# A decoder layer with 60 experts: the shared expert's second product is moved from ahead of the expert rounds to behind them

## The chip, the cores and the metric

One core of one Trainium2 chip. The time is that of one execution on the device, in microseconds (us), the median of several runs. All data are float32.

## What is computed

A pre-norm decoder layer on 8 sequences of 100 tokens of width 512: self-attention, cross-attention, and a mixture of experts. The change touches only the last part, where `x` is the normed input, 800 rows of 512:

```python
gu = x @ se_gate_up_w.T                       # shared expert, 2 x 1408 hidden
shared = silu(gu[:, :1408]) * gu[:, 1408:] @ se_down_w.T
shared = shared * sigmoid(x @ shared_gate_w.T)
weights, sel = top_k(softmax(x @ gate_w.T), 4)   # of 60 experts
for e in range(60):                           # 352 hidden each
    gu_e = x @ w13[e].T
    sparse += cw[:, e] * ((silu(gu_e[:, :352]) * gu_e[:, 352:]) @ w2[e].T)
out = residual + shared + sparse
```

"The second product" of the shared expert is the one with `se_down_w` (1408 to 512).

## The kernel before

The kernel is written engine by engine: each has one block of instructions in a fixed order, and they meet by semaphores alone. `L1120` is line 1120 of the kernel. After the attention part (two sequences a turn, four turns) come these stages.

**Shared expert, first product.** `shared_up(u)` on PE (L1062) for 22 units (11 chunks of 128 hidden by 2 halves of 400 tokens); ACT takes the silu (L1375), DVE multiplies into `hT_all` (L1884). Its weights `se_up` come in 11 loads by SP into three buffers (`load_up`, L471). Beside it DVE chooses the experts and gives each token a row in `xs_d` (`choose`, `sort`, `slots`); when `slots_ready` is given (L1872), POOL scatters the normed rows from `xn3` to `xs_d` with 32 indirect transfers (L727).

**Shared expert, second product.** PE waits for `sh_h`, `down_loaded`, `slots_ready`. With `w_down` as the weights and `hT_all` as the moving side it makes 8 groups (2 halves by 4 chunks of the output) of 11 matmuls, each of which the trace counts as two (L1120). ACT copies each group to `dnT` (L1422), PE transposes back to rows of tokens (L1114, `down_back`), DVE adds them, times the gate, to `acc` (L1899), which holds the residual. `acc` is loaded by L525 and `w_down` by L526, ahead of the fourth `se_up` load on SP's queue.

**Expert rounds.** 20 rounds of three experts. One has a tile of 128 rows ("single", k = 0), two share a tile, 64 rows each ("pair", k = 1). In a round PE does: gate/up of the pair (L1149), transposes of the next single rows (L1137), down of the single (L1176), transposes of hidden (L1164), gate/up of the next single (L1145), rows transposes, down of the pair (L1180), hidden transposes. Two rounds are one turn of a loop; the first transposes and gate/up stand ahead of it and the last round and a half behind. Experts alternate between two sets s = 0, 1 of three buffers (`w13_s[s][b]`, `w2_s[s][b]`); SP loads an expert in three transfers, 2112 KB together (L532 to L534), when the buffer's last reader is done (`y_full`). ACT loads the rows (L1379) and stores the results (L1399). Before the change PE's first rows transpose waits for DVE's adds (`dn_free`, L1201), and SP's `load_pair(1, 1)` waits for `dn_full` (L548), since these buffers lie over `hT_all`. Experts with more rows than a tile would go through an overflow block with a counter (L1219 and its like on the other engines); in this data it runs no turn.

**Gather.** POOL fetches the four result rows of each token with 32 indirect transfers (L738), into four slots of `xn3` that are free again when DVE has added them to `acc` with the token's weights (L1957). After the four of one sequence SP stores it (L576).

**Memory.** All of this lies in one arena of 51250 floats a partition, laid out by hand: `carve` gives out space, and resetting `top[0]` lays one tile over another.

Of the kernel before, what the change touches and what calls it, by code (L numbers as in the profile page):

```python
# [13 lines left out]
P = 128  # L14
# [106 lines left out]
def decoder_kernel(nc, x, ctxT, dcaT, W_attn, W_out, b_out, Wq, bq, Wkv, bkv, Wdca, bdca, norm, Wo, bo,  # L121
# [6 lines left out]
    with cm:  # L128
# [123 lines left out]
        xsT = [carve(DC, T) for _ in range(2)]  # L252
        s_sh = [carve(400) for _ in range(2)]
        xn3 = carve(B, D)
        oh = carve(B, E)
# [10 lines left out]
        w2_s[1][0] = carve(3, D)  # L266
        assert top[0] <= B * DC * S + 3 * DC * 2 * P
        top[0] = B * DC * S + 3 * DC * 2 * P
        dnT = arena[:, DC * 2 * I + 3 * D:DC * 2 * I + 3 * D + DC * 400].rearrange("p (a b) -> p a b", a=DC)
        assert DC * 2 * I + 3 * D + DC * 400 <= B * DC * S + 3 * DC * 2 * P  # L270
        for b in (1, 2):
            w13_s[1][b] = carve(DC, 2 * I)
            w2_s[1][b] = carve(3, D)
        assert top[0] <= B * DC * S + 3 * DC * 2 * P + MC * B * S
        top[0] = B * DC * S + 3 * DC * 2 * P + MC * B * S
# [3 lines left out]
        y_s = [carve(D) for _ in range(2)]  # L279
        top[0] = xs_at  # L280
# [73 lines left out]
        dn_full = sem("shared_down_full")  # L354
        dn_free = sem("shared_down_free")
        r_act = sem("router_exp")
# [60 lines left out]
        def _(sp):  # L417
# [146 lines left out]
            with sp.If(count > 0):  # L564
                with sp.Fori(0, NOV) as t:
                    with sp.If(count > t):
                        e = sp.value_load(ov_i[0:1, bass.ds(t, 1)], min_val=0, max_val=E - 1)
                        sp.wait_ge(o_y, t + 1)
                        sp.sem_inc(load_gate, 1)
                        sp.dma_start(w13_s[0][0], w13[e, :, :, :]).then_inc(o_w, 16)  # L570
                        sp.dma_start(xs_s[0][0], xs_d[bass.ds(t * T + TILES * T, T), :]).then_inc(o_w, 16)
                        sp.dma_start(w2_s[0][0][:, 0:2, :], w2[e, 0:256, :].rearrange("(p c) n -> p c n", c=2)).then_inc(o_w, 16)
                        sp.dma_start(w2_s[0][0][0:96, 2, :], w2[e, 256:I, :]).then_inc(o_w, 16)
            for b in range(B):
# [168 lines left out]
        def _(pe):  # L743
# [362 lines left out]
            pe.wait_ge(sh_h, UNITS)  # L1106
            pe.wait_ge(down_loaded, 16)
            pe.wait_ge(slots_ready, 1)

            def down_back(half):  # L1110
                pe.wait_ge(dnT_copied, 4 * (half + 1))
                for b in range(half * 4, half * 4 + 4):
                    for d in range(DC):
                        last = nc.tensor.transpose(ps[0:S, b, d * P:(d + 1) * P], dnT[:, d, (b % 4) * S:(b % 4 + 1) * S], ident[:])  # L1114
                    last.then_inc(dn_full, 1)

            for half in range(2):
                for d in range(DC):
                    for m in range(MC):
                        last = nc.tensor.matmul(ps[:, half * 4 + d, 0:400], w_down[:, m, d * P:(d + 1) * P],  # L1120
                                                hT_all[:, m, half * 400:(half + 1) * 400], start=(m == 0), stop=(m == MC - 1))
                    last.then_inc(dnT_full, 1)
                    if (half, d) == (1, 0):
                        down_back(0)
            down_back(1)


# [91 lines left out]
            with pe.If(count > 0):  # L1219
                with pe.Fori(0, NOV) as t:  # L1220
                    with pe.If(count > t):
                        pe.wait_ge(o_w, t * 64 + 64)
                        pe.wait_ge(o_yc, t + 1)
                        rows_products(xs_s[0][0]).then_inc(o_t, 1)
                        pe.wait_ge(o_tc, t + 1)
                        gate_up_products(0, 0).then_inc(o_g, 1)
# [3 lines left out]
                        down_products(0, 0).then_inc(o_y, 1)  # L1230


        @block.scalar
        def _(act):
# [181 lines left out]

            for half in range(2):
                for d in range(DC):
                    act.wait_ge(dnT_full, half * 4 + d + 1)
                    if half:  # L1420
                        act.wait_ge(dn_full, 4)
                    nc.scalar.activation(dnT[:, d, :], ps[:, half * 4 + d, 0:400], ACT.Copy).then_inc(dnT_copied, 1)  # L1422

            silu(0, 0)
# [15 lines left out]
            with act.If(count > 0):  # L1440
                with act.Fori(0, NOV) as t:
                    with act.If(count > t):
                        act.wait_ge(o_g, t + 1)
                        silu_part(0).then_inc(o_s, 1)
                        act.wait_ge(o_y, t + 2)
                        act.wait_ge(o_st, t * 16 + 1)
                        nc.scalar.activation(y_s[0], ps[:, 6, :], ACT.Copy).then_inc(o_yc, 1)
                        act.wait_ge(o_yc, t + 2)
                        act.dma_start(ys_d[bass.ds(t * T + TILES * T, T), :], y_s[0]).then_inc(o_st, 16)


        @block.vector
        def _(dve):
# [441 lines left out]

            dve.wait_ge(acc_loaded, 16)
            for b in range(B):
                dve.wait_ge(dn_full, b + 1)
                nc.vector.scalar_tensor_tensor(out=acc[0:S, b, :], in0=ps[0:S, b, :], scalar=rsm[0:S, 6, b, 2:3],  # L1899
                                               in1=acc[0:S, b, :], op0=ALU.mult, op1=ALU.add).then_inc(dn_free, 1)  # L1900

            def rows_T(k, turn):
# [40 lines left out]
            with dve.If(count > 0):  # L1943
                with dve.Fori(0, NOV) as t:
                    with dve.If(count > t):
# [5 lines left out]
                        hidden_T_part(0).then_inc(o_htc, 1)  # L1951
            dve.wait_ge(dn_free, B)
            for b in range(B):
                for k in range(TOPK):
                    n = b * TOPK + k
                    dve.wait_ge(gathered[n % 4], 16 * (n // 4 + 1))
                    ins = nc.vector.scalar_tensor_tensor(out=acc[0:S, b, :], in0=xn3[0:S, n % 4, :], scalar=rsm[0:S, 5, b, k:k + 1],  # L1957
                                                         in1=acc[0:S, b, :], op0=ALU.mult, op1=ALU.add)
                    ins.then_inc(added[n % 4], 1)
                    dve.wait_ge(added[n % 4], n // 4 + 1)  # L1960
                dve.sem_inc(out_ready, 1)

# [47 lines left out]
```

## Time and profile before

| | us |
|---|---|
| median of 3 timed runs | 1322.32 (1320.95 to 1324.74) |
| the profiled execution, its span | 1337.3 |
| PE busy in it | 1142.7 (85%) |
| first shared product, first to last matmul | 681.2 to 826.3 |
| second shared product | 827.0 to 890.7 |
| expert rounds | 890.5 to 1277.9 |
| gather and output | 1278.6 to 1337.3 |

Engines: PE = TensorE matmul, PEld its weight loads, DVE = VectorE, ACT = ScalarE, POOL = GpSimd, SP = SyncE, which here only issues transfers; "SPq", "ACTq" are the queues' issues. Times are us from the span's start. In brackets behind a row stands how long the engine was idle ahead of it, and what ended that; "issue" is idle time in which it waited for nothing that the profile shows. PEclk is the granted clock of TensorE as a share of 2.4 GHz. The DMA share is the mean busy share of 16 transfer engines; it can pass 1 a little. The profiled execution is 15 us longer than the median of the timed ones.

### The profile page before, as it was taken

What the parts mean: (1) busy time and instruction counts of PE and PEld (TensorE: products, weight loads), DVE (VectorE), ACT (ScalarE), POOL (GpSimd) and SP (SyncE); (2) the same over time, 40 slices, a digit from 0 to 9 for tenths busy, and PEclk for the clock granted to TensorE, in tenths of its full rate; (3) what the DMA queues carried; (4) which work ended last, traced back from release to release, by engine and by line L of the source; (5) the groups of instructions that cost most, each with busy time, mean ns of one, the idle gap of its engine ahead of it and who ended that gap; (6) DMA issues with size and microseconds to landing.
All of it is one profiled execution on the core that took longest, in us unless ns stands there. A gap on an engine that the chain in (4) does not pass through costs nothing.

```text
span 1337.3 us, 19386 instructions
## 1 busy us (share of the span) xinstructions
PE 1142.7 (85%) x5710; PEld 630.4 (47%) x5710; DVE 495.5 (37%) x1360; ACT 255.0 (19%) x796; POOL 397.3 (30%) x917
## 2 busy tenths in 40 slices
PE   2889899988999899898979988989988989989920
PEld 0444564446644466444645544555444544444500
DVE  7232755337552375525754601012111111211234
ACT  0141421324232241413321100001101110101100
POOL 3677206852088422884000170000000000000045
PEclk8999899899999899998989998999989998989965
DMA  9998001000100001002037286038999999999835
GB/s 313 333 394 308 1 21 32 22 1 2 32 21 22 0 2 50 3 1 85 1 89 193 74 260 229 3 115 327 385 377 375 383 379 382 384 385 387 326 112 149
DMA packets 76439, 232.73 MB, mean 174 GB/s; under 512 B 11346, under 2 KB 13750, under 8 KB 68670
## 3 DMA queue, kind: packets, MB, share of 16 engines
q1 hardware_dynamic: 58686, 197.55, 41.3%
q10 hardware_dynamic: 11520, 20.98, 4.4%
q0 software_dynamic: 6144, 13.13, 3.3%
q8 instruction: 42, 0.69, 0.2%
q14 instruction: 47, 0.39, 0.1%
HBM read 178.40 MB, written 53.22 MB: 173 GB/s over the span
## 4 chain that ended last, share of the span: by engine, by line
PE 46%; POOL 19%; issue 12%; DMA 11%; DVE 6%; SPq 2%; POOLq 2%; ACT 1%; DVEq 0%; ACTq 0%
PE ps L1062 8%; PE ps L1149 7%; PE ps L1145 6%; DMA arena<-in_w 5%; PE ps L1120 4%; POOL arena L667 4%; PE ps L791 4%; PE ps L1180 3%; PE ps L1176 3%; PE ps L946 2%; POOL arena L664 2%; DMA arena<-ys_d,slot_u 2%; DMA arena<-in_se_up 2%; POOL arena L689 2%; PE ps L926 2%
## 5 line engine op out<-in xcount | busy, mean ns | idle before, releaser
L791 PE MATMUL ps<-arena 128*100 128x512 f32 (+3 forms) x576 | 221.4, 537 | 6.3 <-ACT arena L1247 3.7
L738 POOL DMA_INDIRECT arena<-ys_d,slot_u x32 | 35.0, 1095 | 492.0 <-issue 487.5
L791 PEld LDWEIGHTS ps<-arena 128*100 128x100 f32 (+1 forms) x576 | 90.9, 178 | 114.0 <-issue 108.3
L1149 PE MATMUL ps<-arena 128*64 128x352 f32 x640 | 116.9, 525 | 29.0 <-issue 25.9
L1062 PE MATMUL ps<-arena 128*128 128x400 f32 x352 | 125.0, 514 | 15.6 <-issue 8.3
L873 PE MATMUL ps<-arena 128*100 128x512 f32 x256 | 114.5, 592 | 0.0
L1905 DVE COPY arena<-ps 128x512 f32<-128x512 f32 x40 | 27.7, 691 | 232.8 <-PE ps L1137 232.8
L1062 PEld LDWEIGHTS ps<-arena 128*128 128x128 f32 x352 | 68.4, 195 | 70.8 <-issue 20.5
L1145 PE MATMUL ps<-arena 128*128 128x352 f32 x320 | 98.0, 459 | 1.7 <-issue 1.7
L1149 PEld LDWEIGHTS ps<-arena 128*64 128x64 f32 x640 | 55.4, 156 | 82.9 <-issue 60.6
L1300 ACT ACTIVATE arena<-ps,arena 100x345 f32<-100x345 f32 x128 | 69.2, 546 | 113.4 <-DVE arena L1697 111.8
L1145 PEld LDWEIGHTS ps<-arena 128*128 128x128 f32 x320 | 59.2, 190 | 31.6 <-issue 1.9
L873 PEld LDWEIGHTS ps<-arena 128*100 128x100 f32 x256 | 42.0, 166 | 59.7 <-issue 57.3
L1697 DVE TENSOR_REDUCE arena<-ps 100x1 f32<-100x345 f32 x128 | 60.8, 507 | 24.0 <-PE ps L917 23.5
L946 PE MATMUL ps<-zero 128*128 128x200 f32 x320 | 67.3, 342 | 0.0
L1392 ACT ACTIVATE arena<-ps 128x352 f32<-128x352 f32 x40 | 18.6, 464 | 238.3 <-PE ps L1149 145.6
L727 POOL DMA_INDIRECT xs_d<-arena,slot_u x32 | 31.9, 997 | 100.3 <-DVE ov_i L1872 90.9
L1701 DVE COPY arena<-ps 115x400 f32<-115x400 f32 x92 | 52.4, 569 | 23.4 <-PE ps L926 23.0
L667 POOL TENSOR_TENSOR arena<-arena 115x256 f32<-115x256 f32 (+7 forms) x128 | 57.8, 452 | 10.0
L926 PE MATMUL ps<-ident,arena 100*115 100x100 f32 x384 | 52.4, 273 | 9.3 <-DVE arena L1701 9.1
L1120 PE MATMUL ps<-arena 128*128 128x400 f32 x176 | 59.5, 500 | 0.7 <-DVE arena L1884 0.7
L1180 PE MATMUL ps<-arena 128*64 128x512 f32 (+1 forms) x240 | 56.0, 601 | 0.7 <-DVE arena L1921 0.7
(214 smaller groups left out, 1517.3 us busy)
## 6 DMA issues: line engine op xcount, KB each, us to landing
arena<-in_w SPq DMA_DIRECT2D x60, 1408.0 KB, 11.5
arena<-in_w SPq DMA_DIRECT2D x60, 512.0 KB, 12.1
xs_d<-zero SPq DMA_DIRECT2D x5, 3328.0 KB, 26.3
arena<-in_w SPq DMA_DIRECT2D x60, 192.0 KB, 13.7
arena<-xs_d ACTq DMA_DIRECT2D x40, 256.0 KB, 8.0
ys_d<-arena ACTq DMA_DIRECT2D x40, 256.0 KB, 7.7
ys_d<-zero SPq DMA_DIRECT2D x2, 3328.0 KB, 24.3
arena<-in_se_up SPq DMA_DIRECT2D x11, 512.0 KB
```

Source lines behind the costliest of these rows:

```text
L667: then(nc.gpsimd.tensor_tensor(s3[:, :, 0:w], s3[:, :, 0:w], s3[:, :, w:2 * w], ALU.add))
L791: last = nc.tensor.matmul(ps[0:m, k, 0:cols[1] - cols[0]], lhs(c), w[:, c, cols[0]:cols[1]], start=(c == 0), stop=(c == n_c - 1))
L873: last = nc.tensor.matmul(ps[0:S, j, :], cT[c % 2][:, g, :], w_out[:, c * G + g, :], start=(c == 0 and g == 0), stop=(c == KV - 1 and g == ...
L926: last = nc.tensor.transpose(ps[0:LC, k, r * S:(r + 1) * S], xp[(4 * t + r) % NP_][0:S, c * LC:(c + 1) * LC], ident[0:S, 0:S])
L946: nc.tensor.matmul(ps[:, 6 + j, 0:2 * S], zero[:, 0:P], zero[:, 0:2 * S], start=False, stop=False)
L1062: last = nc.tensor.matmul(ps[:, (u % 3) * 2 + gu, 0:400].rearrange("p (a b) -> p a b", a=4), se_w[m % 3][:, c, gu * P:(gu + 1) * P], tok, ...
L1120: last = nc.tensor.matmul(ps[:, half * 4 + d, 0:400], w_down[:, m, d * P:(d + 1) * P], hT_all[:, m, half * 400:(half + 1) * 400], start=(m ...
L1145: last = nc.tensor.matmul(ps[:, 1 + gu, 0:I], xsT[0][:, c, :], w13_s[s][0][:, c, at:at + I], start=(c == 0), stop=(c == DC - 1))
L1149: last = nc.tensor.matmul(ps[half * HALF:(half + 1) * HALF, 3 + gu, 0:I], xsT[1][:, c, half * HALF:(half + 1) * HALF], w13_s[s][1 + half][ ...
L1180: last = nc.tensor.matmul(ps[half * HALF:(half + 1) * HALF, 7, :], hT[1][0:w, n, half * HALF:(half + 1) * HALF], w2_s[s][1 + half][0:w, n, :],
L1300: nc.scalar.activation(xp[(4 * t + r) % NP_][0:S, :], ps[0:S, k, 0:LM], ACT.Exp, bias=xnm[0:S, j, h:h + 1], scale=1.0, accum_out=xsum[0:S, ...
L1697: nc.vector.tensor_reduce(xnm[0:S, j, h:h + 1], ps[0:S, k, 0:LM], AX, ALU.max, negate=True).then_inc(xmax_ready.sem, 1)
```

## The change

The second product with its transposes moves on PE behind the rounds and the overflow block; ACT's copies to `dnT` move likewise. DVE's `acc` additions of it are interleaved with the gathered ones: image b's gathered rows, then the shared part of image b - 4, and at the end those of 4 to 7. `dn_free` is gone. The loads: `acc` goes out behind the last expert's load, `w_down` once both `y_full` say that round 18 is done. In the arena, `w_down` now lies over set 0's buffers (the single's, and the start of the first pair buffer); the set 1 pair buffers move off `hT_all`: one has space of its own, the other lies over `s_sh` and `xn3`. So `load_expert(1, 1, ...)` can go out at once behind the first round's, and `load_expert(1, 2, ...)` when all units of `sh_h` are done and all rows are scattered. The overflow block uses set 1's single buffer instead of set 0's. Arithmetic and the number of instructions are the same.

```diff
@@ arena
+        xT3_end = top[0]
         hT_all = carve(MC, B * S)
-        w_down = carve(MC, D)
         acc = carve(B, D)
+        down_at = top[0]
         for b in range(3):
             w13_s[0][b] = carve(DC, 2 * I)
             w2_s[0][b] = carve(3, D)
+        w13_s[1][1] = carve(DC, 2 * I)
+        w2_s[1][1] = carve(3, D)
...
+        top[0] = xn3_at
+        w13_s[1][2] = carve(DC, 2 * I)
+        w2_s[1][2] = carve(3, D)
+        assert top[0] <= xn3_end
+        top[0] = down_at
+        w_down = carve(MC, D)
@@ sync
             sp.dma_start(xn3[0:S], xn3_d.rearrange("b s d -> s b d")).then_inc(xn3_loaded, 16)
-            sp.dma_start(acc[0:S], x2_d.rearrange("b s d -> s b d")).then_inc(acc_loaded, 16)
-            sp.dma_start(w_down, se_down.rearrange("(c p) n -> p c n", p=P)).then_inc(down_loaded, 16)
             for m in range(3, MC):
                 load_up(m)
...
             load_pair(0, 0)
+            load_expert(1, 1, 2 + SINGLES)
+
             sp.wait_ge(sh_up, UNITS)
             load_single(1, 1)
-            sp.wait_ge(dn_full, B)
-            load_pair(1, 1)
+
+            sp.wait_ge(sh_h, UNITS)
+            sp.wait_ge(scattered, 16 * B * TOPK)
+            load_expert(1, 2, 2 + SINGLES + 1)
             with sp.Fori(0, ROUNDS // 2 - 1) as ii:
...
+
+            sp.dma_start(acc[0:S], x2_d.rearrange("b s d -> s b d")).then_inc(acc_loaded, 16)
+
+            sp.wait_ge(y_full[0], ROUNDS)
+            sp.wait_ge(y_full[1], ROUNDS)
+            sp.dma_start(w_down, se_down.rearrange("(c p) n -> p c n", p=P)).then_inc(down_loaded, 16)
@@ tensor
             pe.wait_ge(sh_h, UNITS)
-            pe.wait_ge(down_loaded, 16)
             pe.wait_ge(slots_ready, 1)
-            def down_back(half):
...
-            down_back(1)
@@
-            pe.wait_ge(dn_free, 4)
             transpose_rows(0, 0, 0, 0)
             gate_up(0, 0, 0, 0)
             transpose_rows(1, 0, 0, 0)
-            pe.wait_ge(dn_free, B)
             transpose_hidden(0, 0)
@@ behind the overflow block
+            pe.wait_ge(down_loaded, 16)
+            def down_back(half):
...
+            down_back(1)
@@ vector, behind the overflow block
-            dve.wait_ge(dn_free, B)
-            for b in range(B):
+            dve.wait_ge(acc_loaded, 16)
+
+            def add_gathered(b):
                 for k in range(TOPK):
...
+            def add_shared(b):
+                dve.wait_ge(dn_full, b + 1)
+                nc.vector.scalar_tensor_tensor(out=acc[0:S, b, :], in0=ps[0:S, b, :], scalar=rsm[0:S, 6, b, 2:3],
+                                               in1=acc[0:S, b, :], op0=ALU.mult, op1=ALU.add).then_inc(out_ready, 1)
+
+            for b in range(B):
+                add_gathered(b)
+                if b >= 4:
+                    add_shared(b - 4)
+            for b in range(4, B):
+                add_shared(b)
```

## Rows read from the trace of the kernel before

**Rows 1.** The page's slices: busy tenths in 40 equal slices.
```profile
PE   2889899988999899898979988989988989989920
DMA  9998001000100001002037286038999999999835
```

**Rows 2.** Busy time by stretch (columns: PE, PEld, DVE, ACT, POOL; clock, DMA, GB/s).
```profile
850.00:900.00 50.00, 46.37 (x168) 27.89 (x166) 7.23 (x12) 2.99 (x7) 0.00 (x0) 1.00 0.15 56
905.00:910.00 5.00, 5.00 (x21) 2.98 (x20) 1.80 (x5) 1.06 (x2) 0.00 (x0) 1.00 0.33 91
1200.00:1250.00 50.00, 46.92 (x212) 24.49 (x212) 9.87 (x29) 5.90 (x11) 0.00 (x0) 0.97 1.03 381
1265.00:1270.00 5.00, 4.08 (x29) 2.40 (x31) 0.62 (x2) 0.59 (x1) 0.00 (x0) 1.00 0.19 67
1300.00:1338.00 38.00, 0.00 (x0) 0.00 (x0) 16.52 (x22) 0.00 (x0) 21.94 (x20) 0.50 0.52 147
```

**Rows 3.** The chain that ended last, from 690 us on (start, length, what).
```profile
702.39 24.70 DMA arena<-in_se_up
...
826.40 0.58 DVE arena L1884
827.03 37.21 PE ps L1120 x110
...
865.99 22.18 PE ps L1120 x66
...
888.75 1.95 PE ps L1114 x16
...
1333.64 0.75 DVE arena L1957
```

**Rows 4.** Timeline of PE, 665 to 850 us: the unit behind the rank products.
```profile
727.13 5.64 PE L1062 MATMUL ps<-arena 128*128 128x400 f32 x16 [0.45 <-DMA arena<-in_se_up]
```

**Rows 5.** Timeline around the start of the expert rounds.
```profile
823.65 1.83 ACTq L1379 DMA_DIRECT2D arena<-xs_d  x4
...
889.43 2.73 DVE L1899 SCALAR_TENSOR_TENSOR arena<-ps,arena 100x512 f32<-100x512 f32 x4 [21.91 <-PE ps L1114]
...
892.85 4.97 PE L1145 MATMUL ps<-arena 128*128 128x352 f32 x16 [1.72 <-issue]
```

**Rows 6.** The tile xs_d, 800 to 900 us: its six row loads.
```profile
DMA to landing us min/median/max: 2.6/4.1/8.8
```

**Rows 7.** Timelines of SP and of PE in the expert rounds.
```profile
909.48 0.35 SPq L532 DMA_DIRECT2D arena<-in_w  x1
...
917.40 0.34 SPq L532 DMA_DIRECT2D arena<-in_w  x1
...
934.18 4.95 PE L1149 MATMUL ps<-arena 128*64 128x352 f32 x32 [0.50 <-DMA arena<-in_w]
...
993.52 7.35 PE L1149 MATMUL ps<-arena 128*64 128x352 f32 x32 [3.72 <-issue]
...
1252.16 0.34 SPq L534 DMA_DIRECT2D arena<-in_w  x1
```

**Rows 8.** PE's waits, 905 to 1275 us (total, times, longest).
```profile
PE ps L1149 <- issue: 25.9, 10, 3.7
```

**Rows 9.** Timeline of the end of the rounds and the first gather.
```profile
1275.11 2.80 PE L1180 MATMUL ps<-arena 128*64 128x512 f32 x12 [0.71 <-DVE arena L1921]
...
1282.53 1.05 POOL L738 DMA_INDIRECT arena<-ys_d,slot_u  x1 [479.58 <-issue]
```

**Rows 10.** By stretch again, while acc and w_down are loaded.
```profile
704.00:706.00 2.00, 2.00 (x7) 1.13 (x6) 0.78 (x3) 1.63 (x4) 0.00 (x0) 1.00 0.96 200
718.00:720.00 2.00, 2.00 (x26) 2.00 (x24) 0.88 (x3) 0.00 (x0) 0.00 (x0) 1.00 0.92 345
```

**Rows 11.** The load of w_down: from issue to landing.
```profile
DMA to landing us min/median/max: 32.2/32.2/32.2
```

**Rows 12.** Timeline of DVE, 740 to 905 us, around the engine stall.
```profile
806.88 1.13 DVE L1884 TENSOR_TENSOR arena<-arena,ps 128x400 f32<-128x400 f32 x2 [22.64 <-remote]
```

More of the change, by code:

```diff
@@ L252, in decoder_kernel @@
         xsT = [carve(DC, T) for _ in range(2)]
+        xn3_at = top[0]
         s_sh = [carve(400) for _ in range(2)]
         xn3 = carve(B, D)
+        xn3_end = top[0]
         oh = carve(B, E)
@@ L260, in decoder_kernel @@
         rsm = carve(8, B, 8)
-        top[0] = 0
-        w13_s[1][0] = carve(DC, 2 * I)
[L266 to L275, printed above, removed]
         sl = [carve(I) for _ in range(2)]
@@ L279, in decoder_kernel @@
         y_s = [carve(D) for _ in range(2)]
+        top[0] = 0
+        w13_s[1][0] = carve(DC, 2 * I)
+        w2_s[1][0] = carve(3, D)
+        dnT = carve(DC, 400)
+        assert top[0] <= xT3_end
+        top[0] = xn3_at
[4 more added lines that the diff above has]
+        w_down = carve(MC, D)
         top[0] = xs_at
@@ L354, in decoder_kernel @@
         dn_full = sem("shared_down_full")
-        dn_free = sem("shared_down_free")
         r_act = sem("router_exp")
@@ L1106, in _ @@
             pe.wait_ge(sh_h, UNITS)
-            pe.wait_ge(down_loaded, 16)
             pe.wait_ge(slots_ready, 1)
-            def down_back(half):
[L1111 to L1124, printed above, removed]
-            down_back(1)
             def transpose_rows(k, s, turn, j):
@@ L1229, in _ @@
                         pe.wait_ge(o_htc, t + 1)
-                        down_products(0, 0).then_inc(o_y, 1)
+                        down_products(0, 1).then_inc(o_y, 1)
+                        pe.wait_ge(o_yc, t + 2)
+            pe.wait_ge(down_loaded, 16)
+            def down_back(half):
+                pe.wait_ge(dnT_copied, 4 * (half + 1))
+                for b in range(half * 4, half * 4 + 4):
+                    for d in range(DC):
+                        last = nc.tensor.transpose(ps[0:S, b, d * P:(d + 1) * P], dnT[:, d, (b % 4) * S:(b % 4 + 1) * S], ident[:])
+                    last.then_inc(dn_full, 1)
+            for half in range(2):
+                for d in range(DC):
+                    for m in range(MC):
+                        last = nc.tensor.matmul(ps[:, half * 4 + d, 0:400], w_down[:, m, d * P:(d + 1) * P],
+                                                hT_all[:, m, half * 400:(half + 1) * 400], start=(m == 0), stop=(m == MC - 1))
+                    last.then_inc(dnT_full, 1)
+                    if (half, d) == (1, 0):
+                        down_back(0)
+            down_back(1)
         @block.scalar
@@ L1415, in round_ @@
                 store(1, i)
[L1417 to L1422, printed above, removed]
             silu(0, 0)
@@ L1449, in _ @@
                         act.dma_start(ys_d[bass.ds(t * T + TILES * T, T), :], y_s[0]).then_inc(o_st, 16)
+            for half in range(2):
+                for d in range(DC):
+                    act.wait_ge(dnT_full, half * 4 + d + 1)
+                    if half:
+                        act.wait_ge(dn_full, 4)
+                    nc.scalar.activation(dnT[:, d, :], ps[:, half * 4 + d, 0:400], ACT.Copy).then_inc(dnT_copied, 1)
         @block.vector
@@ L1894, in _ @@
             run(router)
-            dve.wait_ge(acc_loaded, 16)
-            for b in range(B):
-                dve.wait_ge(dn_full, b + 1)
-                nc.vector.scalar_tensor_tensor(out=acc[0:S, b, :], in0=ps[0:S, b, :], scalar=rsm[0:S, 6, b, 2:3],
-                                               in1=acc[0:S, b, :], op0=ALU.mult, op1=ALU.add).then_inc(dn_free, 1)
             def rows_T(k, turn):
@@ L1951, in _ @@
                         hidden_T_part(0).then_inc(o_htc, 1)
-            dve.wait_ge(dn_free, B)
-            for b in range(B):
+            dve.wait_ge(acc_loaded, 16)
+            def add_gathered(b):
                 for k in range(TOPK):
@@ L1956, in _ @@
                     dve.wait_ge(gathered[n % 4], 16 * (n // 4 + 1))
-                    ins = nc.vector.scalar_tensor_tensor(out=acc[0:S, b, :], in0=xn3[0:S, n % 4, :], scalar=rsm[0:S, 5, b, k:k + 1],
-                                                         in1=acc[0:S, b, :], op0=ALU.mult, op1=ALU.add)
-                    ins.then_inc(added[n % 4], 1)
+                    nc.vector.scalar_tensor_tensor(out=acc[0:S, b, :], in0=xn3[0:S, n % 4, :], scalar=rsm[0:S, 5, b, k:k + 1],
+                                                   in1=acc[0:S, b, :], op0=ALU.mult, op1=ALU.add).then_inc(added[n % 4], 1)
                     dve.wait_ge(added[n % 4], n // 4 + 1)
-                dve.sem_inc(out_ready, 1)
+            def add_shared(b):
[8 more added lines that the diff above has]
+                add_shared(b)
 def kernel(x, ctx_1024, L0_attn_W_attn, L0_attn_W_out, L0_attn_b_out, L0_xattn_Wq, L0_xattn_bq, L0_xattn_Wk, L0_xattn_bk,
```

8 lines of the change are left out of this document (4 added, 4 removed).

## The prediction

> **What bounds the kernel now.** I read the slices of the page first, then the table by stretch, then the chain of waits, then the timelines of the places that the change touches. In the 40 slices of 33.4 us [rows 1] the reader is to see two holes: DMA at 0 and 3 in the 26th and 27th slice (836 to 903 us), and PE at 2 and 0 in the last two. By stretch [rows 2], 850 to 900 us has 46.4 us of PE work and 56 GB/s of transfers; 1200 to 1250 has 46.9 us of PE work and 381 GB/s, DMA share 1.03; 1300 to 1338 has no PE work. So three stages in a row have three limits: the shared down product runs on PE alone, the expert rounds run at what the DMA engines carry (with PE close behind), the gather at the end runs on POOL, DMA and DVE with PE empty. The chain goes through all three one after the other. The down product fills 827.03 to 890.70 = 63.7 us of it (110 and 66 matmuls and, between and behind them, two lots of 16 transposes, of which the second has its row) [rows 3], and the first expert row transpose follows at once. Behind the last expert product, which ends at 1277.9, 59.4 us of gather and store remain to the span's end at 1337.3 [rows 9]. The change moves the 63.7 us from a place where PE is the chain to one where PE is idle. In the best case nearly all of it is hidden by the gather; what isn't is the sum below. All instants are those of the profile of before.
>
> **Part 1, the early loads.** SP no longer issues acc (1600 KB) and w_down (2816 KB) at 692.9 to 702.4. Behind them the fourth se_up load was late, but the chain's 24.70 us of DMA [rows 3] is its flight, not PE's wait: PE idled 0.45 us for it [rows 4]. Gain between 0 and 0.5 us; I take 0.
>
> **Part 2, where the rounds start.** After the change PE needs three things for its first transpose: the last hidden (DVE, which starts at 826.40 and takes 0.58 [rows 3]: 827.0), slots_ready (long there: the scatters run on it from 761.6) and its rows. ACT issues the row loads at 823.65 already now, landing in 2.6, 4.1 or 8.8 us (shortest, median, longest of six such loads) [rows 5, 6]: at 826.3, 827.7 or 832.5. I take the median, since the queues are nearly empty then. In the kernel before, the first L1145 came at 892.85, just behind a DVE copy that itself had to wait until the last adds L1899 ended at 889.43 + 2.73 = 892.16 [rows 5]. Now transposes 0.6, copy 0.7, 0.1 of passing on: 827.7 + 1.4 = 829.1. Shift 892.85 - 829.1 = 63.7; with the longest landing 59. Some "issue" idle at this first run through the code is not excluded, so I take 63. SP's added waits are harmless: load (1,1) goes out behind the first three experts, at about 808.5; (1,2) waits for the last hidden and the scatters (POOL's last at 802), so about 828.5. Behind that wait on SP stand only round 2's loads, which need a round to finish first. A pair load issued from 917.40 on was in use at 934.18 with DMA full [rows 7]; (1,2), issued at 828.5, is wanted at about 853.
>
> **Part 3, the rounds.** Before, pair (1,1) went out from 891.45 and was there long before its use at 916.85; the DMA share of 905 to 910 was 0.33 [rows 2], so the queues ran empty before round 2's first load at 909.48 [rows 7]. From there to the end they are full. So loading (1,1) and (1,2) early takes bytes out of a place that had room, and doesn't shorten the full part: 20 rounds keep their length, 0. Bounds: -0.5 (the 0.50 us wait at 934.18 [rows 7]) and +3 (one more loop-head stall like those of [rows 7, 8]). The acc load stands on SP's queue behind the last expert load (issued 1252.2 [rows 7]), and delays none.
>
> **Part 4, the weights of the moved product.** w_down lies over expert buffers of the even rounds, so SP waits for y_full of round 18: L1180 ends at about 1264.9, and the issue follows at 1265.3 to 1265.8. The expert loads drain at about 1265.9 (67 GB/s in 1265 to 1270 is 0.34 MB [rows 2]). Then acc and w_down stand in the queue: 4.52 MB. What they took before: w_down landed 32.2 us after its issue at 693.62 [rows 11], so at 725.8, with xn3 and acc ahead of it; the rate was 200 GB/s at 704 to 706 although the engines' share was 0.96, and 345 at best [rows 10]. The 2 us stretches from 692 on, of which two stand there, add up to the 1.84 MB ahead of acc at about 703.7, so the two took 22.1 us. 1265.9 + 22.1 = 1288. The ends: 1265.9 + 4.52 MB at 381 GB/s [rows 2] = 1277.8, and the full 32.2 us from issue = 1297.5. I take 1287.5, since the nearest row is the same two loads, and se_up traffic that was mixed in then is gone. PE is ready at 1278.6 plus the walk past the overflow block; it waits about 9 us.
>
> **Part 5, the moved product.** 63.7 us of its own [rows 3]; its covers there (ACT copies of 0.5 us behind each group of 22) come with it. PE has been idle 9 us, and its granted clock falls to 0.50 (1.2 GHz) when it idles [rows 2]. At the loop heads the 32 matmuls L1149 behind 3.7 us of idle take 7.35 us, against 4.95 at full clock [rows 7]: +2.4. End of PE: 1287.5 + 63.7 + 2.4 = 1353.6. The last add trails the last transpose by 892.16 - 890.70 = 1.5 [rows 3, 5]; the last output store takes what it takes now, 1337.3 - (1333.64 + 0.75) = 2.9 [rows 3]. End: 1358.0, 20.7 behind the old one.
>
> **Part 6, the gather beside it.** DVE adds the shared part of image b - 4 behind the gathered rows of image b. Images 0 to 4 are gathered by about 1318. dn_full of image 0 comes at 1287.5 + 2.4 + 37.2 + 0.5 = 1327.6, so DVE stands there some 10 us, and queued behind it are images 5 to 7 and POOL's gathers, which go at most four ahead of DVE. The four of image 5 have landed; the eight others need two turns of the ring, each about 6.5 us (four gathers of 1.05 us and 0.3 between them [rows 9], then the last one's landing): 1344 with the adds. That is 9 us before PE ends, so the stall is hidden. What ACT and DVE do for the product costs no more than there: it follows PE. The last y store (256 KB, 2.0 us alone) now shares the engines with w_down; 2 us more there shift the gather only, inside those 9 us.
>
> **Sum.** -63 + 20.7 = -42.3. On the profiled execution 1337.3 - 42.3 = 1295.0. The median of the timed runs is 1322.3, 15.0 below the profiled span. None of my terms rests on what the profiling adds, as far as I can tell, so I carry the difference over: 1322.3 - 42.3 = 1280.0.
>
> **The rivals.**
> (a) The weights land early. If acc and w_down move at the rounds' rate they are there at 1277.8 and PE runs on. That takes 9 us of waiting and 2.4 us of slow clock away, since 0.71 us of idle before L1180 cost no clock (2.80 us, as in the other rounds) [rows 9]; but PE's walk past the overflow block is no longer hidden, priced by the loop heads' 2.9 to 3.7 us of "issue" (25.9 us in ten places, 3.7 the longest) [rows 8]: 1280 - 9 - 2.4 + 3 = about 1272. For: w2 is loaded in short rows too and the rounds reach 381 GB/s. Against: [rows 10], these very transfers.
> The Trainium skill, "DMA: Bandwidth & Descriptors", section "Anatomy of one DMA", gives about 2 us plus bytes over 436 GB/s for one transfer; by it the two would be there near 1278, this rival. No row here shows such a rate for these two.
> The skill's "Runtime: NRT & Kernel Launch", section "Instruction fetch mechanics", says that a taken branch outside the fetched pages stalls the engine; that fits the loop heads' "issue" idle and would count against placing work behind the overflow branch, but only in this rival, where nothing covers it.
> (b) The weights land late, as 32.2 us behind their issue: PE starts at 1297.5, +10: 1290. For: gather and y store share the engines. Against: xn3 isn't ahead of them now.
> (c) The engine stall of 784 to 806 grows. DVE idled 22.64 us there for something "remote", and two hidden products came together at 806.88 [rows 12], where they were due every 5.4 us (16 matmuls at 37.21 / 110 us [rows 3]) behind the one of 783.7, at 789 and 794.5: about 12 us lost, while transfers were dense. The fourth expert load now keeps the queues dense to about 820, and the same may recur there, or in the gather: +12, 1292. For: it coincides with dense transfers. Against: 704 to 706 was dense too (share 0.96 [rows 10]) and PE ran through.
> (d) The same stall goes away, as SP's early transfers are fewer: -12, 1268. For: it isn't in the data flow. Against: the engines' code ahead of it is unchanged.
> (e) Slower: the moved product stays at the low clock. It sits beside the gather, PE starts cold, and at 1.2 GHz for its whole length it takes 127 instead of 66: 1341, 19 us above the old time. It decides from the point where the product takes over 66 + 42 = 108 us. For: the clock is 0.50 all through the gather now. Against: PE is idle there now; behind a loop head 32 matmuls take 7.35 us, not the 9.9 that half the clock would make of all of them [rows 7], so PE gets its clock back within them, and here it starts with denser ones.
> (f) The change doesn't do what it says: the first rounds still wait for something late (rows, or pair (1,2)), and half of the shift is lost: 1311. Against: every releaser I found is there by 832.5.
>
> **How the numbers follow.** Forecast 0.52, (a) 0.14, (b) 0.12, (c) 0.09, (d) 0.07, (e) 0.03, (f) 0.03. The forecast's own spread is 6 us either way (row landing, 4 us; weights within the bounds). The range holds the forecast, (a), (b) and (c) and most of (d): 1265 to 1296. A measurement of this kernel tells about 0.3%, 4 us, from no change. Faster: all but (e) and what of (f) is worse than half: 0.95. Same: 0.02. Slower: 0.03.
>
> **What would show it.** The first L1145 near 829; L1149 of round 0 to 3 with the same spacing as now; the w_down landing 20 to 24 us behind the last expert load's end, and a PE idle of 7 to 11 us put down to it; the product 66 us long with the clock at 0.50 for its first 3 to 5 us; the chain of the last 75 us on PE, not on POOL; DVE idle some 10 us for dn_full after image 4. I am wrong if the rounds get longer, if the gather ends last, or if PE shows "issue" idle inside the product.

## The result, and the profile after

| | us |
|---|---|
| before, median of 4 | 1321.89 (1320.95 to 1324.74) |
| after, median of 4 | 1289.76 (1282.66 to 1291.61) |
| ratio | 0.9743, 95% interval 0.9709 to 0.9777 |
| profiled execution of after, its span | 1286.5 (before: 1337.3) |

The change gains 32.1 us. 42.3 were forecast: 1280.0, range 1265 to 1296. The span of the profiled execution fell by 50.8 us, much more than the median. That gap is the first thing to explain, and a part of the forecast's error lies in it.

I cut each profile at three instants: first L1062 of the shared expert (called L1073 after the change), first gate/up of the rounds (L1145; L1137), end of the last expert product (L1180; L1172).

| profile | first shared matmul at | to first gate/up | rounds | tail | span |
|---|---|---|---|---|---|
| before | 681.2 | 211.7 | 385.0 | 59.4 | 1337.3 |
| after | 675.0 | 148.4 | 387.7 | 75.4 | 1286.5 |
| difference | -6.2 | -63.3 | +2.7 | +16.0 | -50.8 |
| forecast | 0 | -63 | 0 | +20.7 | -42.3 |

By this table the forecast's terms look right, and the start exact to 0.3 us. It isn't: the chain of after shows an item that the forecast didn't have. First the chain (start, length, what; "..." stands where lines are left out):

```profile
727.29 80.81 PE ps L1073 x240
808.19 0.58 DVE arena L1894
808.77 12.73 issue
821.51 1.08 PE ps L1129 x4
...
1193.37 22.07 DMA arena<-in_se_down
...
1215.48 38.90 PE ps L1235 x110
1254.38 1.75 PE ps L1229 x16
1256.13 22.18 PE ps L1235 x66
```

Against [rows 3]: the shared product's last group is followed by 12.73 us in which PE does nothing, put down to "issue". At the end the chain is w_down's load and then the product (L1235), no longer the gather. The engine timelines of the same two places:

```profile
811.99 1.87 ACTq L1389 DMA_DIRECT2D arena<-xs_d  x4
821.51 1.08 PE L1129 MATMUL ps<-ident,arena 128*128 128x128 f32 x4 [13.42 <-issue]
823.42 6.74 PE L1137 MATMUL ps<-arena 128*128 128x352 f32 x16 [0.83 <-issue]
...
1215.48 7.00 PE L1235 MATMUL ps<-arena 128*128 128x400 f32 x15 [4.39 <-DMA arena<-in_se_down]
```

These answer to [rows 5]. ACT's last silu ended at 805.9 and nothing of its own was due, yet it issued the row loads at 811.99: its program waits there for the scatters, and for nothing else. POOL had issued the last of those by 796.8, but in 810 to 812 us seven of their packets (q0) were still moving beside the expert loads (q1); the columns are packets, MB and share:

```profile
q1 hardware_dynamic: 73, 0.60, 92.2%
q0 software_dynamic: 7, 0.02, 2.6%
```

And the row loads themselves took, in 800 to 822 us,

```profile
DMA to landing us min/median/max: 9.3/11.8/12.8
```

where [rows 6] had 2.6, 4.1 and 8.8 (in the same profile the four loads of the start alone took 2.6 to 4.2). So PE's idle is a wait for rows, although the profile doesn't say so. The stretches show why (columns as in [rows 2]):

```profile
800.00:805.00 5.00, 5.00 (x17) 2.81 (x16) 0.57 (x1) 0.50 (x1) 0.00 (x0) 1.00 1.04 408
805.00:810.00 5.00, 3.08 (x10) 1.42 (x8) 0.57 (x1) 0.50 (x1) 0.00 (x0) 1.00 0.98 385
815.00:820.00 5.00, 0.00 (x0) 0.00 (x0) 0.00 (x0) 0.00 (x0) 0.00 (x0) 0.50 1.05 352
825.00:830.00 5.00, 5.00 (x15) 2.93 (x15) 0.00 (x0) 0.00 (x0) 0.00 (x0) 0.80 0.02 8
```

The transfer engines are full from 785 to 825, and PE idles inside that; when PE works again they are empty. PE's clock fell to 0.50, so the first gate/up took 6.74 us instead of 4.97 [rows 5].

### The profile page after: what moved, and what is told of

The parts are those of the page before. It is cut to its first block, busy times and chain, and to the rows that moved or that the text cites. A ratio compares the mean times of both kernels' runs of the same rounds, so it can differ in the third digit from the quotient of the medians.

```text
span 1286.5 us, 19385 instructions
## 1 busy us (share of the span) xinstructions
PE 1141.3 (89%) x5710; PEld 627.8 (49%) x5710; DVE 496.4 (39%) x1360; ACT 254.3 (20%) x796; POOL 394.6 (31%) x917
## 3 DMA queue, kind: packets, MB, share of 16 engines
q1 hardware_dynamic: 58686, 197.55, 42.3%
## 4 chain that ended last, share of the span: by engine, by line
PE 48%; POOL 18%; issue 12%; DMA 11%; DVE 6%; SPq 2%; POOLq 2%; ACT 1%; DVEq 0%; ACTq 0%
PE ps L1073 9%; PE ps L1141 7%; DMA arena<-in_w 6%; PE ps L1137 6%; PE ps L1235 5%; POOL arena L678 4%; PE ps L802 4%; PE ps L1172 3%; PE ps L1168 3%; PE ps L957 3%; POOL arena L675 2%; POOL arena L700 2%; PE ps L937 2%; DMA arena<-in_se_down 2%; POOL arena L689 2%
## 5 line engine op out<-in xcount | busy, mean ns | idle before, releaser
L1141 PE MATMUL ps<-arena 128*64 128x352 f32 x640 | 117.2, 527 | 29.8 <-issue 15.1
L1073 PE MATMUL ps<-arena 128*128 128x400 f32 x352 | 122.0, 509 | 6.6 <-DMA arena<-xT_d 5.7
L1137 PE MATMUL ps<-arena 128*128 128x352 f32 x320 | 99.8, 466 | 0.8 <-issue 0.8
L1073 PEld LDWEIGHTS ps<-arena 128*128 128x128 f32 x352 | 67.9, 194 | 59.3 <-issue 8.5
L1141 PEld LDWEIGHTS ps<-arena 128*64 128x64 f32 x640 | 53.5, 157 | 85.7 <-issue 71.7
L1137 PEld LDWEIGHTS ps<-arena 128*128 128x128 f32 x320 | 60.2, 193 | 31.7 <-issue 2.7
L1402 ACT ACTIVATE arena<-ps 128x352 f32<-128x352 f32 x40 | 18.5, 463 | 254.3 <-PE ps L1141 146.5
L1235 PE MATMUL ps<-arena 128*128 128x400 f32 x176 | 61.2, 510 | 4.4 <-DMA arena<-in_se_down 4.4
L738 POOL DMA_INDIRECT xs_d<-arena,slot_u x32 | 31.8, 995 | 100.5 <-DVE ov_i L1882 91.1
L1172 PE MATMUL ps<-arena 128*64 128x512 f32 (+1 forms) x240 | 56.0, 601 | 0.7 <-DVE arena L1925 0.7
```

Source lines behind the costliest of these rows:

```text
L1073: last = nc.tensor.matmul(ps[:, (u % 3) * 2 + gu, 0:400].rearrange("p (a b) -> p a b", a=4), se_w[m % 3][:, c, gu * P:(gu + 1) * P], tok, ...
L1137: last = nc.tensor.matmul(ps[:, 1 + gu, 0:I], xsT[0][:, c, :], w13_s[s][0][:, c, at:at + I], start=(c == 0), stop=(c == DC - 1))
L1141: last = nc.tensor.matmul(ps[half * HALF:(half + 1) * HALF, 3 + gu, 0:I], xsT[1][:, c, half * HALF:(half + 1) * HALF], w13_s[s][1 + half][ ...
L1172: last = nc.tensor.matmul(ps[half * HALF:(half + 1) * HALF, 7, :], hT[1][0:w, n, half * HALF:(half + 1) * HALF], w2_s[s][1 + half][0:w, n, :],
```

## The experiments

All ratios are against the kernel before, run on the same chip. "start" is the time from the first shared matmul to the first gate/up, "wait" PE's idle before the moved product. (1,0), (1,1) and (1,2) are the three experts of round 1: the single and the two of the pair. "1/11 product" leaves out ten of the eleven chunks of the second product.

| run | ratio (95% interval) | start | rounds | tail | wait | span |
|---|---|---|---|---|---|---|
| before, again | 1.0008 (0.997 to 1.0047) | 200.1 | 384.4 | 56.9 | | 1318.3 |
| before, 1/11 product | 0.9583 (0.952 to 0.9646) | 146.3 | 380.9 | 59.8 | | 1261.7 |
| after, again | 0.974 (0.9716 to 0.9765) | 144.6 | 383.6 | 78.8 | 8.2 | 1282.4 |
| after, 1/11 product | 0.9651 (0.9594 to 0.9708) | 145.4 | 384.2 | 64.9 | 3.5 | 1270.9 |
| rows first | 0.9698 (0.9624 to 0.9772) | 136.0 | 387.8 | 80.0 | 8.0 | 1282.0 |
| (1,1) behind the scatters | 0.9727 (0.9699 to 0.9756) | 135.3 | 389.7 | 78.0 | 6.6 | 1281.7 |
| (1,0), (1,2) behind the rows | 0.9706 (0.9684 to 0.9729) | 141.2 | 377.6 | 78.9 | 7.4 | 1274.8 |
| acc early | 0.9683 (0.965 to 0.9715) | 148.6 | 380.7 | 71.4 | 2.1 | 1276.5 |
| acc early, again | 0.969 (0.9653 to 0.9727) | 149.1 | 381.0 | 71.4 | 2.1 | 1279.6 |
| rows first, acc early | 0.9722 (0.9699 to 0.9745) | 136.0 | 397.4 | 71.3 | 2.1 | 1281.2 |
| (1,0), (1,2) behind the rows, acc early | 0.9726 (0.97 to 0.9753) | 141.6 | 396.5 | 72.9 | 2.1 | 1287.6 |
| (1,1) behind the scatters, acc early | 0.9722 (0.9686 to 0.9758) | 134.8 | 398.8 | 72.9 | 2.1 | 1279.4 |

**1. Was the profile of before a usual one?** The kernel before, unchanged.

> The kernel before, unchanged, for a second profile. Theory S (the profile on which the prediction rested carried a stall of the engines of about 12 us at 784 to 806, and some 6 us more ahead of it, which the timed runs don't have): the span is 1318 to 1325 now, DVE has no idle of 22.64 us for something remote in the first shared product, and from the first L1062 matmul to the first L1145 of the rounds it takes about 199 us, not 211.6. Theory N (the stall belongs to the kernel before, and the 10 us missing from the forecast are lost elsewhere): span near 1337, 211.6 us again. The ratio is 1 by both.

Measured: span 1318.3, start 200.1 us. Theory S holds for the start: 11.6 us of the 211.7 in the profile on which the forecast rests were a stall that this execution lacks. The 56 timed executions of the kernel before lie between 1313.9 and 1332.4 us, and in every later run the profiled span is 1.8 to 2.1 us below the time of the same execution. So the 1337.3 us were an unusually long execution, and not something that profiling adds. ACT, PE and the stretches at the hand-over, in this second profile of before:

```profile
807.81 0.50 ACT L1375 ACTIVATE arena<-ps 128x400 f32<-128x400 f32 x1 [4.87 <-PE ps L1062]
809.17 1.83 ACTq L1379 DMA_DIRECT2D arena<-xs_d  x4
811.19 29.15 PE L1120 MATMUL ps<-arena 128*128 128x400 f32 x86 [0.73 <-DVE arena L1884]
```
```profile
800.00:805.00 5.00, 5.00 (x17) 2.81 (x16) 0.39 (x1) 0.50 (x1) 0.00 (x0) 1.00 1.01 405
805.00:810.00 5.00, 5.00 (x17) 2.77 (x15) 0.57 (x1) 0.50 (x1) 0.00 (x0) 1.00 0.35 137
```

The reader is to see that the queues run dry at about 807 and the rows are issued at 809.17, 2 us later. In the first profile the stall of [rows 12] had held PE and ACT back by 12 us while the transfers went on, so the rows went out at 823.65 [rows 5] into queues empty since 815. When nothing stalls, the kernel has 2 us of such margin. The second product hid that too: PE needs the rows only 64 us later.

**2. What the product cost where it stood.** Before, with one chunk of eleven (the rest is left out); `range(MC)` becomes `range(1)` in the loop around L1120.

> The kernel before with the second shared product cut to 1 of its 11 chunks of hidden (16 matmuls instead of 176; its transposes, copies and adds stay). Part of the computation is left out. It measures what PE's time there is worth where it stood. If all of it is on the path, 160 matmuls at 0.338 us = 54 us are gained: ratio 0.959, and everything behind is as before. Theory Q (transfers hold the start of the rounds once the product is gone) says the same here, since 9 us of transposes and copies are left as cover: between 48 and 54. A gain under 45 would say that the rounds can't start earlier at all.

Measured: 56.1 us less (1265.94 against 1322.06), against 54 of matmul time; start 146.3 instead of 200.1, 53.8 less. All of what was left out was on the path, and a start of 146 us was reached with transposes, copies and adds still in it, and three early experts instead of four.

**3. What it costs where it stands now.** The same cut in the changed kernel.

> The changed kernel with the same cut, 1 of 11 chunks, where the product stands now, behind the rounds. Part of the computation is left out. If the gather hides most of the product, the end falls back to the gather: tail from the last expert product to the end 59.4 us as before plus some 3 us for a gather that starts later behind w_down, so 62 to 63 instead of 75.4: 13 us less than the changed kernel, ratio 0.965. If nothing is hidden (PE's work there holds the gather up by the adds), 54 us less: 0.934.

Measured: 1275.1, 14.7 us below the changed kernel's 1289.8 in its own runs and about 10.7 below its second series (1285.8); the tail is 64.9 us against 75.4 and 78.8. So of the 54 us, 11 to 15 show behind the rounds and 39 to 43 are hidden by the gather. 62 to 63 were expected for the tail; 64.9 came. POOL's first gather starts 6.0 us behind the last expert product (1212.04 against 1206.0), where it took 4.6 before: the last y store shares the engines with w_down. The other runs bear that out: 6.0 to 8.1 us in the six profiles with acc behind the rounds, and 4.6 in the five with acc early (experiments 6 and 7), where w_down had landed before the last expert product ended.

**4. Scatters, rows and expert loads at the start of the rounds.** SP issues round 1's experts only when the first rows are there:

```diff
-            load_expert(1, 1, 2 + SINGLES)
             sp.wait_ge(sh_up, UNITS)
-            load_single(1, 1)
             sp.wait_ge(sh_h, UNITS)
             sp.wait_ge(scattered, 16 * B * TOPK)
+            sp.wait_ge(xs_loaded[1][0], 16)
+            load_single(1, 1)
+            load_expert(1, 1, 2 + SINGLES)
             load_expert(1, 2, 2 + SINGLES + 1)
```

> The changed kernel, but SP issues the three experts of round 1 only when the rows of round 0 have landed (waits on the last hidden, the scatters and the row load of the pair). Theory Q (the 13.4 us of PE idle ahead of the rounds are scatters and row loads that wait among dense expert transfers): 2.16 MB less stand beside the scatters and 4.3 MB less beside the rows, so ACT's row loads go out at about 806 instead of 812 and land in 3 to 4 us; PE starts 9 to 11 us earlier, ratio 0.967 to 0.969. Theory F (the idle is the engines' own stall at new code, not the transfers): no change, ratio 0.976. Against it: if the experts of round 1 now come late, PE waits for them in round 1 and the gain is lost there.

Measured: start 136.0, 12.4 us less. ACT and PE, and PE's waits from 830 us on:

```profile
809.85 1.83 ACTq L1388 DMA_DIRECT2D arena<-xs_d  x4
812.76 0.63 PE L1128 MATMUL ps<-ident,arena 128*128 128x128 f32 x4 [1.48 <-DVE arena L1893]
```
```profile
PE ps L1140 <- DMA arena<-in_w: 27.7, 8, 4.5
PE ps L1234 <- DMA arena<-in_se_down: 8.0, 1, 8.0
```

The 13.4 us of idle became 1.5, and ACT issued 0.7 us behind its last silu instead of 6.1: theory Q is shown, theory F is out. But the median is 1284.6, and the ratio 0.9698 isn't clear of the changed kernel's. Counted from the first shared matmul, the end came at 603.8 us, against 611.5 and 607.0 in the two profiles of the changed kernel: 12.4 or 8.6 us gained at the start, 7.7 or 3.2 left at the end. PE's waits put down to expert weights grew from 14.7 and 18.6 to 27.7 us, and the wait for w_down is as long as ever. About half was given back. The transfers that the start no longer carries are made up in the rounds: 387.8 us at a mean of 376 GB/s are 146 MB, against 387.7 us at 363 GB/s, 141 MB, in the changed kernel. So the column "rounds" doesn't compare like with like where experts are loaded later.

**5. Which of the loads does it.** Expert (1,1) alone moved behind the scatters, `load_expert(1, 1, ...)` next to (1,2):

> The changed kernel, but expert (1,1) is loaded behind the scatters, together with (1,2), instead of ahead of them; (1,0) stays at the end of the first shared product. Theory Q1 (the fourth early expert delays the scatters, and ACT's row loads wait for these): the row loads go out at about 809 instead of 812. They still stand behind (1,0) and beside two more experts, so they land 9 to 11 us later: PE starts about 3 us earlier, and first shared product to first gate/up takes 145 us instead of 148.4. If the fourth expert alone were the cause, 136 as in the run where all three wait.

Measured: 135.3, not 145. My split was wrong. Without the fourth expert the scatters end at about the same time as ACT's last silu (809.0); the rows go out at 809.60, ahead of SP's (1,0) at 811.86, and the two terms vanish together:

```profile
809.60 1.84 ACTq L1388 DMA_DIRECT2D arena<-xs_d  x4
...
812.59 0.63 PE L1128 MATMUL ps<-ident,arena 128*128 128x128 f32 x4 [1.48 <-DVE arena L1893]
```

The other way round, (1,1) early and (1,0), (1,2) behind the rows:

> The changed kernel, but (1,0) and (1,2) are issued when the pair's first rows have landed; (1,1) goes out early as in the changed kernel. Theory Q2 (the row loads themselves stand among expert transfers): they go out at 812 as now, since the scatters are still late, but land in 3 to 4 us instead of 9 to 13; PE starts about 6 us earlier: 142 us instead of 148.4.

Measured: 141.2. The rows, still issued late behind the scatters (813.62, 5.6 us behind the last silu), land in 2.6, 3.6 and 4.5 us instead of 9.3, 11.8 and 12.8, and PE's idle is 6.2 us instead of 13.4:

```profile
816.43 1.09 PE L1129 MATMUL ps<-ident,arena 128*128 128x128 f32 x4 [6.22 <-issue]
```

Both halves are shown: the fourth early expert delays the scatters, for which the rows wait, and then the loads (1,0) and (1,2) delay the rows. The first causes the second. All profiles agree on the first half: ACT issues the rows 5.2 to 7.4 us behind its last silu in the seven with (1,1) early, and 0.1 to 0.7 in the four with (1,1) later.

**6. The load of acc.** Back at its old place, behind xn3; only w_down stays behind the rounds.

> The changed kernel with the acc load back at its old place, behind xn3; only w_down is loaded behind the rounds. Theory D (the end of the rounds is bound by transfers up to the landing of w_down, acc being part of them): w_down lands 14 to 15 us behind its issue instead of 22.1, so it is there before PE needs it: PE's 4.4 us of wait and some 2 us of slow clock go, 5 to 6 us less than the changed kernel, ratio 0.970. The early acc costs 0.5 us at most. If w_down's landing doesn't depend on acc: no change.

> The changed kernel with the acc load at its old place, a second time: the one step beside the change that looked better than it (0.9683), and a second profile of it. The profiles so far have a pace of the rounds from 19.05 to 20.2 us at 366 to 390 GB/s, with 19.15 in the first run of this kernel and 19.9 to 20.2 in its three relatives that also load acc early. If the pace belongs to the kernel: 19.1 to 19.2 us again, rounds of 380 us, ratio 0.967 to 0.969. If it belongs to the execution: anywhere in that span, and the ratio between 0.968 and 0.973; the tail is 71 to 72 us with a product wait of 2 us by both, since that is what acc early changes.

Measured, twice: w_down lands 11.9 and 11.6 us behind its issue instead of 22.1, PE waits 2.1 us both times (put down to "issue"; I take it for PE's own walk past the overflow block, which rival (a) priced at 3), and the tail is 71.4 us both times. Ratios 0.9683 and 0.969; medians 1278.1 and 1279.8. In the first profile PE's wait, and the time to landing of w_down:

```profile
PE ps L1234 <- issue: 2.1, 1, 2.1
```
```profile
DMA to landing us min/median/max: 11.9/11.9/11.9
```

By its medians this is the best kernel of the study, some 6 to 12 us below the changed one. The intervals overlap (0.9653 to 0.9727 and 0.9716 to 0.9765 in the second pair), so I take the sign as likely, and as shown only the 4 to 7 us of the tail.

**7. Do the two steps add up?** Three combinations of 4, 5 and 6.

> Both: round 1's experts behind the first rows, and acc early. In the run with the rows first alone, PE started the rounds 12.4 us earlier, but waited 8.0 us for w_down at the end instead of 4.4, and rounds had 27.7 us of waits for weights instead of 14.7. Theory D: without acc these 8 us are gone, 1284.6 - 8 = 1277, ratio 0.964, better than both kernels. If the end is bound by other transfers, w_down lands as late as now and the ratio stays 0.970.

> The changed kernel with (1,0) and (1,2) behind the first rows, (1,1) early, and acc at its old place. Apart these gave starts of 141.2 us (instead of 148.4) and a product wait of 2.1 us (instead of 4.4) with a ratio of 0.9706 and 0.9683. If they add up: start 141, wait 2, ratio 0.963 to 0.966, better than both kernels. If the end of the rounds is set by the bytes to move from 777 on (the transfers never pause, so an earlier start of PE only turns into waits for weights), it stays at 0.968 to 0.970, as with acc early alone.

> The changed kernel with (1,1) behind the scatters and acc at its old place. Start 135 us (measured apart), product wait 2. If starts and tails add up freely, ratio 0.960 to 0.963. By the bytes theory the earlier start is given back in the rounds, as in the run with the rows first and acc early (397 us of rounds at 369 GB/s instead of 388 us at 384): 0.968 to 0.972.

They don't. Starts of 136.0, 141.6 and 134.8 and waits of 2.1 came as expected, but the rounds took 397.4, 396.5 and 398.8 us, and the ratios are 0.9722, 0.9726 and 0.9722. The pace of the transfers in 920 to 1190 us, changed kernel, rows first with acc early, and acc early again, in this order:

```profile
920.00:1190.00 270.00, 246.22 (x1115) 125.59 (x1112) 49.61 (x139) 29.22 (x55) 0.00 (x0) 0.94 1.02 386
```
```profile
920.00:1190.00 270.00, 238.86 (x1086) 122.47 (x1082) 47.98 (x133) 28.36 (x54) 0.00 (x0) 0.95 1.02 376
```
```profile
920.00:1190.00 270.00, 247.98 (x1123) 126.50 (x1122) 50.45 (x140) 29.69 (x56) 0.00 (x0) 0.95 1.02 390
```

The engines' share is 1.02 in all three; what differs is the bytes they move in it, 376 against 386 and 390 GB/s. Over 920 to 1180 us the three combinations moved 371 to 376 GB/s, and the nine other profiles that I compared 381 to 392. The share stands at its full value throughout, and the shortest rounds go with the highest rate and the longest with the lowest (377.6 us at 392, 398.8 at 371), so I hold that the transfers bound the rounds; in between the order is loose (389.7 us at 382, but 384.4 at 381). Why the rate is some 4% lower in the three combinations, and not with acc early alone (392 and 391), stays open: I have one profile of each. It isn't the chip: the changed kernel moved 386 GB/s on the one on which two of the three had 373 and 371. A smaller loss beside it: in two of the three the first 110 matmuls of the product took 38.90 us, as in the changed kernel, and 37.21 in the third and in both runs of acc early, behind the same 2.1 us of idle; that makes up the 1.5 us by which their tails are longer.

**8. The changed kernel again.**

> The changed kernel, unchanged, for a second profile and a longer comparison. Theory Q: the 13 us of PE idle ahead of the rounds are there again (first shared product to first gate/up 147 to 149 us), row loads land in 9 to 13 us, the product starts 3 to 5 us behind the last expert product. The pace of the rounds is the transfers': 19.2 to 19.6 us a round at 380 to 388 GB/s; it varies from run to run. If the idle were a stall of one profile only, it would be gone here: 136.

Measured: start 144.6 and rows landing in 6.8, 10.9 and 13.0 us, PE idle 10.3 us; the wait is there again, if 3 us shorter. The product waited 8.2 us for w_down, nearer to my 9 than the first profile's 4.4, since PE had no stall ahead of the last round this time.

## Why the prediction was right, and where it was off

**The bound and the direction** were right: the second product was on the path in full (experiment 2) and some three quarters of it are hidden behind the rounds (experiment 3).

**Part 1, early loads: 0.** PE's 0.45 us wait for se_up behind the rank products is gone. acc costs nothing there: it can stand there again without loss at the start (148.6 and 149.1 against 148.4).

**Part 2, the start: mis-sized, and the step that failed.** I took the row loads at 4.1 us "since the queues are nearly empty then", and called SP's added waits harmless. What I costed of the fourth expert load was whether it would be in time, not what it would do to the transfers beside it: 2.16 MB, 5.7 us at the rate of [rows 2], ahead of the last scatters. The rows went out 6.1 us behind ACT's last silu (in the second profile of before 0.9) and landed in 9.3 to 12.8 us: PE idled 13.4 us for them. [rows 2] and [rows 6] could not show this, because they come from an execution in which the stall of [rows 12] had drained the queues.

**Part 2 came out at the forecast number by cancellation.** -63.3 in the two profiles = -11.6 (a stall that only the first had; rival (d) on the profile) and -51.7 (from 200.1 to 148.4, the change). The move takes off what I said, and PE's new wait for rows (13.4 us, and a slow clock behind it) puts about a fifth of it back. That the two nearly cancel in the table is luck.

**The sum.** I carried the profile's 15 us over the median to both sides, with the words "None of my terms rests on what the profiling adds, as far as I can tell". One did: the start. And profiling added nothing; the execution was a long one (experiment 1). Against the undisturbed profile of before, the change is -51.7 at the start, +3.3 in the rounds, +18.5 in the tail, -1.9 ahead of all that: 1318.3 - 31.8 = 1286.5. That is within 0.3 us of the measured 32.1; with the second profile of after (1282.4) it would be 35.9, so an agreement this close is luck too.

**Part 3, the rounds: 0, bounds -0.5 to +3.** +2.7 and, in the second profile of after, -1.4. Right; but "they keep their length" has a reverse that I didn't draw: when transfers bound the rounds, an earlier start is worth only what the transfers can use. Experiment 4 shows it: 8.6 to 12.4 us at the start, 3.2 to 7.7 at the end.

**Part 4, the weights: 20 to 24 us behind the end of the expert loads.** w_down landed 22.1 us behind its issue, 20.8 in the second profile, and 20.0 to 22.5 in the six with acc behind the rounds; the forecast has 22.0 from issue to landing. Right, and [rows 10, 11] were the right rows; rival (a), the rounds' rate, is out: at a full share only 221 GB/s moved while they were loaded (columns as in [rows 2]),

```profile
1195.00:1200.00 5.00, 3.31 (x12) 1.67 (x14) 0.00 (x0) 0.00 (x0) 0.00 (x0) 0.56 1.04 221
```

PE's wait was 4.4 and 8.2 us for 9 forecast: in the first profile a stall of 2.93 us and a slow L1141 before the last round took the rest. The Trainium skill's formula in "DMA: Bandwidth & Descriptors", section "Anatomy of one DMA", is fitted there to transfers that GpSimd issues, and these are SP's, which the prediction didn't say; as an estimate it gives 8.6 us for w_down alone. Here 11.6 and 11.9 were measured with next to nothing of SP's ahead of it, and 22.1 with acc.

**Part 5, the product: 66.1 us.** 1215.48 to the end of the last transpose at 1280.85 = 65.4. The first 110 matmuls took 38.90 us instead of 37.21, so the cold start cost 1.7 us, not 2.4; rival (e) is out. The last add ended 1.5 us behind the transposes, as forecast.

**Part 6, the gather.** DVE stood 7.2 us for the first shared part behind image 4, and 6.8 us at the end for PE, so the gather was done 6.8 us before PE (I had 9) and was hidden:

```profile
1254.93 0.75 DVE L1968 SCALAR_TENSOR_TENSOR arena<-ps,arena 100x512 f32<-100x512 f32 x1 [7.17 <-PE ps L1229]
...
1271.99 0.75 DVE L1968 SCALAR_TENSOR_TENSOR arena<-ps,arena 100x512 f32<-100x512 f32 x1
1279.57 2.73 DVE L1968 SCALAR_TENSOR_TENSOR arena<-ps,arena 100x512 f32<-100x512 f32 x4 [6.83 <-PE ps L1229]
```

**The rivals.** (f) was the nearest to what happened, "the first rounds still wait for something late (rows, ...)", and I gave it 0.03 because every releaser that I found was there by 832.5; I had counted releasers, not what stands in front of them. (c), a stall at the dense transfers, gave +12 for another reason. The forecast's own spread was 6 us, and the time came 9.8 us above it; the range held it only because of (b) and (c), neither of which happened as told.

## What to carry to other kernels

A stage that looks like pure cost may be the cover of transfers started before it. When it is taken away, ask what its successor reads, when that was issued and what stands in the queues beside it, and let that load go ahead of the prefetches that aren't due for another round. And before costing from a profile whose span is 15 us over the timed median, find where the 15 us sit, and count them out of the terms that touch them.

## What the runs showed of the hardware

- Four row loads of 256 KB on ACT's queue land in 2.6 to 4.5 us when no expert load is under way (experiment 5, the second run), and in 9.3 to 12.8 us when SP's were issued ahead and beside them (the changed kernel). The Trainium skill, "DMA: Bandwidth & Descriptors", section "Queues, rings and completion order", has each engine take turns between the queues packet by packet. The trace agrees: in 790 to 805 us of the changed kernel SP's queue (q1) and POOL's scatters (q0) moved 809 and 811 packets. But turns by packet are not equal ones in bytes: these were 4.43 and 1.74 MB, so 5.5 and 2.1 KB a packet. A small load on a queue of its own isn't protected by it: the fastest row load needed 9.3 us, in which at 352 to 359 GB/s some 3.3 MB moved, about one and a half experts:

```profile
q1 hardware_dynamic: 809, 4.43, 71.7%
q0 software_dynamic: 811, 1.74, 29.9%
```
- With the share at 1.02 the rate in the rounds was anything from 371 to 392 GB/s, which is 10 us and more on their length. What sets it stayed open.
- A stall of some 12 us for something "remote" [rows 12] was in one profile of before and in none of the thirteen others. It held DVE, ACT and PE, but not POOL, which went on issuing scatters every 1.3 us through it. What it was stayed open.
